# A gated graph update on one core: the new state as (1-z)n + zh, shared out over GpSimd, ScalarE and VectorE

## The reference, cut to what matters

```python
h = x
for i in range(4):
    hw = einsum('bnc,cd->bnd', h, weight[i])
    m  = einsum('bjn,bjd->bnd', adj, hw)
    gx = m @ w_ih[i].T + b_ih[i];  gh = h @ w_hh[i].T + b_hh[i]
    r = sigmoid(xr + hr);  z = sigmoid(xz + hz)
    n = tanh(xn + r * hn)
    h = (1 - z) * n + z * h
out = layernorm(x + h * mask[:, :, None])
```

## Time and profile before

| | us |
|---|---|
| median of 3 runs | 537.22 (536.68 to 537.37) |
| the profiled execution | 537.31 |
| its span (first to last instruction) | 535.5 |

### The profile page before, as it was taken

The page is one execution under the profiler, slowest core; times in us unless marked ns, Lnnn a source line. Parts: engine busy times, 40 slices in busy tenths (PEclk is TensorE's granted clock), DMA queues, the critical chain, the costliest instruction groups (busy, mean ns, idle before and its releaser), DMA issues.

```text
span 535.5 us, 7420 instructions
## 1 busy us (share of the span) xinstructions
PE 514.2 (96%) x2288; PEld 422.0 (79%) x2288; DVE 388.8 (73%) x678; ACT 383.8 (72%) x638; POOL 219.9 (41%) x162
## 2 busy tenths in 40 slices
PE   5999999999999999999999999999999999999970
PEld 4688888888888888888888888888888888888760
DVE  3787666666788886666689886667688887767595
ACT  4668777648776779956786877984986777985444
POOL 2045232344345454432336644332355454344443
PEclk9999999999999999999999999999999999999995
DMA  8951653265642356273662166356472165424212
GB/s 305 380 199 47 226 195 126 87 169 156 234 141 80 121 179 226 88 224 119 203 239 77 61 211 215 118 163 190 133 280 80 60 218 171 171 89 151 86 60 82
DMA packets 78896, 85.13 MB, mean 159 GB/s; under 512 B 3768, under 2 KB 61712, under 8 KB 78864
## 3 DMA queue, kind: packets, MB, share of 16 engines
q1 hardware_dynamic: 78864, 84.73, 47.9%
HBM read 64.27 MB, written 20.45 MB: 158 GB/s over the span
## 4 chain that ended last, share of the span: by engine, by line
PE 91%; SPq 2%; DMA 1%; POOL 1%; DVE 1%; issue 1%; ACT 1%; POOLq 0%; DVEq 0%; ACTq 0%
PE p_S L508 40%; PE p_r L522 5%; PE p_r L518 5%; PE p_r L519 5%; PE p_z L518 5%; PE p_z L522 5%; PE p_z L519 5%; PE p_hn L518 3%; PE p_hn L522 3%; PE p_hn L519 3%; PE p_xn L522 3%; PE p_xn L518 3%; PE p_xn L519 3%; DMA adj_in<-in_adj_dram 1%; PE p_tr L453 1%
## 5 line engine op out<-in xcount | busy, mean ns | idle before, releaser
L1272 POOL TENSOR_TENSOR work<-hT,work 128x512 f32<-128x512 f32 x63 | 86.6, 1375 | 266.7 <-ACT work L710 266.7
L508 PE MATMUL p_S<-adj_hi,nat_hi 128*128 128x512 f32 x480 | 187.4, 391 | 0.0
L508 PE MATMUL p_S<-adj_hi,nat_lo 128*128 128x512 f32 x480 | 186.8, 389 | 0.0
L508 PEld LDWEIGHTS p_S<-adj_hi,nat_hi 128*128 128x128 f32 x480 | 90.1, 188 | 18.9 <-DVE nat_lo L894 0.3
L508 PEld LDWEIGHTS p_S<-adj_hi,nat_lo 128*128 128x128 f32 x480 | 90.1, 188 | 18.5
L1141 DVE SCALAR_TENSOR_TENSOR work<-p_hn,bias,work 128x512 f32<-128x512 f32 x62 | 46.5, 750 | 79.3 <-ACT work L710 78.8
L1276 POOL TENSOR_TENSOR work<-work 128x512 f32<-128x512 f32 x63 | 90.1, 1430 | 4.9
L710 ACT ACTIVATE work<-p_r,bsum 128x512 f32<-128x512 f32 x63 | 43.4, 688 | 60.7 <-PE p_r L522 60.6
L931 DVE STREAM_TRANSPOSE work<-hT 128x512 f32<-128x512 f32 x62 | 69.2, 1116 | 2.1
L710 ACT ACTIVATE work<-work,bias 128x512 f32<-128x512 f32 x63 | 45.7, 725 | 31.0 <-DVE work L1145 28.6
L682 ACT ACTIVATE low_words<-adj_in 128x1024 bf16<-128x1024 uint16 x64 | 67.1, 1049 | 1.0
(11 more groups left out here) (148 smaller groups left out, 924.8 us busy)
## 6 DMA issues: line engine op xcount, KB each, us to landing
adj_in<-in_adj_dram SPq DMA_DIRECT2D x72, 512.0 KB, 6.7
bounce<-work SPq DMA_DIRECT2D x62, 256.0 KB, 2.0
low<-bounce SPq DMA_DIRECT2D x62, 256.0 KB, 2.8
x_in<-in_x_dram SPq DMA_DIRECT2D x8, 512.0 KB, 6.7
y<-in_x_dram SPq DMA_DIRECT2D x8, 512.0 KB, 4.4
out_dram<-y SPq DMA_DIRECT2D x7, 512.0 KB, 4.1
out_dram<-y SPq DMA_DIRECT2D x2, 256.0 KB, 2.7
y<-in_L_gnn_w_ih_dram SPq DMA_DIRECT2D x2, 192.0 KB, 7.4
```

What stands on the lines that cost most here:

```text
L508: last = nc.tensor.matmul(p_S[h][:, :], part[:, s, j], adj_hi[:, s, j, half(h)], start=(j == 0 and part is nat_hi), stop=(j == NB - 1 and ...
L1272: nc.gpsimd.tensor_tensor(t_sb[:, h], hT[:, s, half(h)], n_sb[:, h], ALU.subtract).then_inc(d_sub, 1)
```

## The change

In all steps but the last of the last pair, POOL makes zh (into `r_sb`, which is free after `t_mul`) as soon as z and t are there; ACT turns z into 1 - z in place, behind n and zh (`keep`, a Copy with scale -1 and bias 1); and DVE makes (1-z)n into `t_sb` and adds zh. The last step's half 0 keeps its three POOL operations, and one layer-norm power is issued after the loop instead of at its end.

```diff
+            def keep(p, k, h):
+                act.wait_ge(zh_made, HS * p + k + 1)
+                act.wait_ge(n_act, HS * p + k + 1)
+                nc.scalar.activation(z_sb[:, h], z_sb[:, h], ACT.Copy, bias=1.0, scale=-1.0).then_inc(z_kept, 1)
...
                         gate(n_sb[:, h], t_sb[:, h], t_add, n_act, ACT.Tanh, bias[:, 0, G * l + 2:G * l + 3], p, k)
+                        keep(p, k, h)
...
             def new_state(p, g, h):
-                dve.wait_ge(d_mul, HS * p + 2 * g + h + 1)
-                nc.vector.tensor_tensor(hT[:, g % 2, half(h)], n_sb[:, h], t_sb[:, h], ALU.add).then_inc(h_new, 1)
+                dve.wait_ge(z_kept, HS * p + 2 * g + h + 1)
+                nc.vector.tensor_tensor(t_sb[:, h], z_sb[:, h], n_sb[:, h], ALU.mult).then_inc(nz_made, 1)
+                dve.wait_ge(nz_made, HS * p + 2 * g + h + 1)
+                dve.wait_ge(zh_made, HS * p + 2 * g + h + 1)
+                nc.vector.tensor_tensor(hT[:, g % 2, half(h)], r_sb[:, h], t_sb[:, h], ALU.add).then_inc(h_new, 1)
...
-                        pool.wait_ge(n_act, HS * p + k + 1)
-                        nc.gpsimd.tensor_tensor(t_sb[:, h], hT[:, s, half(h)], n_sb[:, h],
-                                                ALU.subtract).then_inc(d_sub, 1)
-
-                        pool.wait_ge(d_sub, HS * p + k + 1)
-                        nc.gpsimd.tensor_tensor(t_sb[:, h], z_sb[:, h], t_sb[:, h],
-                                                ALU.mult).then_inc(d_mul, 1)
...
+                        pool.wait_ge(z_act, HS * p + k + 1)
+                        pool.wait_ge(t_mul, HS * p + k + 1)
+                        nc.gpsimd.tensor_tensor(r_sb[:, h], z_sb[:, h], hT[:, s, half(h)], ALU.mult).then_inc(zh_made, 1)
                     if g in (1, 2) and not first:
                         inverse_deviation(p - 1, g - 1)
-                    elif g == STEPS - 1 and last:
-                        inverse_deviation(p, 0)
 
             pairs(pool, body)
+            inverse_deviation(PAIRS - 1, 0)
```

More of the change, by code:

```diff
@@ L166, in gnn_kernel @@
         d_mul = sem("d_mul")
+        zh_made = sem("zh_made")
+        z_kept = sem("z_kept")
+        nz_made = sem("nz_made")
         h_new = sem("h_new")
@@ L1265, in body @@
                                                     hT_lo[:, s, half(h)].bitcast(F32), ALU.add).then_inc(xT_whole, 1)
-                    for h in range(1 if last and g == STEPS - 1 else 2):
+                    if last and g == STEPS - 1:
+                        pool.wait_ge(n_act, HS * p + 2 * g + 1)
+                        nc.gpsimd.tensor_tensor(t_sb[:, 0], hT[:, 1, half(0)], n_sb[:, 0], ALU.subtract).then_inc(d_sub, 1)
+                        pool.wait_ge(d_sub, 1)
+                        nc.gpsimd.tensor_tensor(t_sb[:, 0], z_sb[:, 0], t_sb[:, 0], ALU.mult).then_inc(d_mul, 1)
+                        pool.wait_ge(d_mul, 1)
+                        nc.gpsimd.tensor_tensor(hT[:, 1, half(0)], n_sb[:, 0], t_sb[:, 0], ALU.add).then_inc(h_new, 1)
+                        break
+                    for h in range(2):
                         k = 2 * g + h
```

## The result

The changed kernel takes 551.64 us (median of 3 runs, 551.37 to 552.01) against 537.22 before: the ratio is 1.0266 with a 95% interval of 1.0249 to 1.0283. The forecast of 549.0 was 2.6 us short, and its range of 540 to 556 holds the time. The profiled execution took 551.64 with a span of 549.8, which is 14.3 more than the 535.5 of before, at the same granted clock (0.988).

What follows compares the result with a forecast made beforehand. PE, busy 96% of the span, was taken as the bound, so lateness of DVE or ACT costs PE time. Terms 5.1 + 1.95 + 2.8 + 1.2 + 0.45 + 0.2 = 11.7 on 537.3 gave 549.0 us, range 540 to 556.

Steps and rivals of the forecast that it cites:

- the hold: DVE's `nat_lo`, with two SBUF inputs, stands behind POOL's running zh: 0.49 us lost for each half.
- A: Steps 4 and 5 of pairs 1 to 3, where ACT is full: 3 x 1.7 = 5.1 us, lower bound 2.7.
- B: Step 0 of pairs 1 to 3: one `keep` in ACT's gapless queue, 0.66 us a time, 1.95 in all.
- C: Step 1, no slack at `hT_lo`: 0.8 us in three pairs, 0.4 in pair 0, 2.8 in all.
- D: Steps 2 and 3 of pairs 1 to 3: DVE's additions against `S_lo`'s slack, 0.2 us a step, 1.2 in all.
- E: Step 7 of pairs 0 to 2: ACT late at `t_mul` of half 0, 0.15 us each, 0.45 in all.
- F: The end: longer `new_state`, and the residual before the last `S_lo` later but under POOL's operations as before: 0.2 us.
- My own case: The forecast's main case, the summed slowdown: 545.5 to 552.5 us, chance 0.50.
- Slack takes more: Rival: same places, but overlooked idle time in each queue absorbs more; 543 us, down to 538.4, chance 0.22.
- The relief on DVE decides: Rival: POOL leaves the residuals and PE's 3.0 us of DVE waits go; faster, 534.3 us, chance 0.07.
- Covered after all: Rival: DVE and ACT, some 80% busy, absorb the work and PE's waits stay; 537.3 us, chance 0.08.
- The power holds DVE: Rival: POOL's layer-norm power holds DVE's product and addition, making steps 2 and 3 cost 9.6; 557 us, chance 0.10.

Runs made afterwards that it cites:

- experiment 2: The changed kernel with the product (1-z)n made on POOL, so that DVE only adds: 542.07 us, ratio 1.009.
- experiment 3: The changed kernel with zh over 8 of 512 columns, most of zh left out, every wait kept: 543.83 us, ratio 1.0114.
- experiment 1: The changed kernel without the Copy on ACT; DVE makes (z-1)n in one instruction and subtracts it from zh: 547.58 us, ratio 1.0187.
- experiment 4: The kernel before with an in-place copy of z added on ACT behind every n: 541.57 us, ratio 1.008.
- experiment 7: The changed kernel without the Copy (DVE makes (z-1)n) and with zh over 8 of 512 columns: 538.84 us, ratio 1.0031.
- experiment 9: The kernel before with full zh added on POOL, its difference and product cut to 8 columns except in the last step: 537.31 us, ratio 1.0003.
- experiment 10: The changed kernel without the Copy (DVE makes (z-1)n), zh of half 1 waiting for the new state of half 0: 540.56 us, ratio 1.0059.
- experiment 5: The kernel before with two DVE moves: step 0's `measure` behind the first residual, the last step's `s_low` ahead of the second: 536.50 us, ratio 0.9994.
- experiment 8: The kernel before with full zh added on POOL ahead of its two old operations, unread, DVE's addition waiting for it: 557.57 us, ratio 1.0386.
- experiment 6: The changed kernel with the two DVE moves of experiment 5: 549.08 us, ratio 1.0224.
- experiment 11: The kernel of experiment 10 with the two DVE moves of experiment 5: 539.73 us, ratio 1.0047.

## Why the prediction was right, and where its terms were off

**The mechanism held.** The time is lost in the new waits that were named: for ACT's `S_hi` in steps 4 and 5 and for r in step 4, more for `t_mul` in step 0 and for `hT_lo` in step 1. Not named was a wait of 0.37 to 0.43 for `hT_lo` in step 0. PE has the same 2288 matmuls, but its busy time, said to be unchanged, is 8.5 us more: the aggregation's keep their mean of 0.391 and 0.389, while those behind the new waits are longer in the record (the one with `S_lo` into `p_r` 0.407 for 0.391). Experiments 2, 3 and 1 take away DVE's product, the hold and the Copy, one each, and give back 9.4, 7.6 and 3.9 of the 14.4 us.

**The prices.** The Copy took 0.63 (0.62 said), the product 0.68 (0.69), the residual of step 1 1.14 (1.13). The hold cost 0.60 instead of 0.49, 1.28 where 0.68 is usual, so that the mean of `nat_lo` is 1.26 and not 1.1 to 1.2. The 0.12 that I let be hidden is there: at `nat_lo`'s start zh still had 208.66 + 1.30 - 209.23 = 0.73 to run, and 0.60 of it was lost. What was off is zh's start. I had it 0.03 behind the end of `t_mul`; it came 0.14 behind (207.77 + 0.75 = 208.52 to 208.66).
The Trainium skill's rule of the whole instruction ("SBUF — State Buffer", section "SBUF: two separate sides") had made 0.61 out of my start. That is close to the 0.60 by chance: from the recorded start it gives 0.73, and the trace shows 0.13 less.

**A**, said 5.1, measured 5.63. Step 4 costs 1.00 to 1.03 instead of 1.25, step 5 0.82 to 0.90 instead of 0.45; that the sum is so near is in part luck, since one is too high and the other too low. The waits in the step 4 shown are 0.48, 0.43 and 0.50 against 0.6, 0.25 and 0.4; the step as a whole gets a part of them back. Step 5 was mis-sized: I took it for a remainder of step 4's lateness, but it has the full ACT queue and both new costs again (0.69 for `S_hi` and 0.43 for `S_lo` in pair 1).

**B**, said 1.95, measured 2.64. "One Copy in ACT's queue" was a cause but not the only one: experiment 4, the Copy alone, costs 1.86 there, and experiment 1, without it, 1.86 as well, by a later `take_xT` that puts `nat_lo<-x_in` under POOL's sum. Experiment 7, with neither, has 0.1. The Copy, or product with hold: either suffices, both together are little more. This step of the prediction was incomplete.

**C**, said 2.8, measured 3.10 (0.66, 0.87, 0.94, 0.63). The saving on the second residual is there (1.14 for 2.17), but the first state product is held by zh as well: it took 1.28 at 290.69. So is the first residual of step 0, 1.67 for 1.13, which the prediction didn't have; in pair 2 it costs nothing, since DVE waits 0.59 for ACT behind it.

**D**, said 1.2 over steps 2 and 3, measured 1.09, all of it in step 3 and none in step 2. **E**, said 0.45, measured 0.51.

**F**, said 0.2, measured 1.64, the term furthest off. 0.60 of it is a wait of 0.94 for `nat_lo` at the last step's start; the same step is as much longer in experiments 1, 2 and 9 (0.56 to 0.60), which have the hold, and no longer in 3, 4 and 7, which don't, nor in 10, where zh comes later. The other 1.04 came through a transfer. The residual ahead of the last `S_lo` waited for it, in DVE's timeline of the last step after:

```profile
530.76 1.14 DVE L957 SCALAR_TENSOR_TENSOR y<-low,mask,y 128x128 f32<-128x128 f32 x4 [3.21 <-DMA low<-bounce]
531.82 0.68 DVE L904 TENSOR_TENSOR S_lo<-p_S,S_hi 128x512 fp32r<-128x512 f32 x1
```

PE's wait for that `S_lo` is 2.83 for the 1.6 of the earlier trace rows. I had that residual as hidden under POOL's three operations, as before, and had the transfers as covered; this one isn't, because a DVE operation that PE waits for stands behind the residual.

**First step and start.** Pair 0's step 0 became 0.60 shorter, the start 0.31 longer: -0.3, not foreseen. It doesn't go with the change: step 0 there is 0.23 to 0.40 shorter in experiments 2, 3, 4, 7 and 9, and 0.24 longer in 10.

**What the sum hid.** I added the three prices at each place, less a slack. The slack is the point. Before, `S_hi` was ready at 213.31 for a load at 214.35, 1.04 of cover. The product's 0.7 alone fits under it, the hold's 0.6 alone too: in step 4 PE's loads wait once only, for r, 0.38 in experiment 7 and 0.24 in experiment 9. But 1.3 doesn't fit, and PEld's timeline in experiment 1 has three waits:

```profile
217.02 0.19 PEld L521 LDWEIGHTS p_r<-S_hi,wx_hi 128*128 128x128 f32 x1 [0.54 <-ACT S_hi L659]
217.75 0.19 PEld L525 LDWEIGHTS p_r<-S_lo,wx_hi 128*128 128x128 f32 x1 [0.43 <-DVE S_lo L903]
219.70 0.19 PEld L521 LDWEIGHTS p_r<-hT_hi,wh_hi 128*128 128x128 f32 x1 [0.50 <-issue]
```

Once `S_hi` is late at all, `S_lo` is late too, by 0.43 in every step 4 and 5 of pairs 1 to 3, here and in the kernel after, whether `S_hi` was late by 0.33 or by 0.70. Step 4 then costs 0.83 to 1.07, step 5 0.5. In step 1 the residual's saved 1.04 is the cover: product or hold alone costs nothing in pairs 1 and 2, both together 0.56 and 0.59. Over all pairs steps 4 and 5 are 4.2 of experiment 1's 10.5, steps 0 of pairs 1 to 3 1.9, steps 1 2.1, the last step and what follows it 2.2. So +1.8 and +0.3 make +10.5 mainly because covers are used up; the part at the end also has a late transfer. The Copy is different: alone it costs 0.45 to 0.71 in step 0, where DVE already stood idle for ACT. I think that with the slack kept apart from the prices A's step 5 would have shown itself; that is an opinion, not a result.

**The range.** My own case was given as 545.5 to 552.5. Its terms, A from 2.7 to 5.8 and a third on each of B to D, make 544.6 to 551.7, and 551.64 is at the upper edge of that: nearly every term was too low. In *Slack takes more*, 1.5 stands for B's 1.95 without a reason.

**The rivals.** *Slack takes more* (543) is refuted by A, B and C at or above their terms. *The relief on DVE decides* (534.3): the residual did get its 1.04 back, but no variant with the product on DVE comes below the kernel before. *Covered after all* is refuted. *The power holds DVE* (557) is refuted in place; POOL's timeline in the kernel after, in step 2 of pair 1:

```profile
199.12 2.01 POOL L1268 TENSOR_TENSOR rstd<-vare,mhalf 128x8 f32<-128x8 f32 x1 [4.42 <-DVE vare L981]
```

and DVE's:

```profile
199.67 0.69 DVE L1003 TENSOR_TENSOR hT<-work 128x512 f32<-128x512 f32 x1
```

The addition has two SBUF inputs, lies wholly under the power and takes its usual 0.69, and so it is at all six powers of steps 1 and 2. `z_rest`, which I had held against this rival, has a single input and was no test of it. The strict reading of the Trainium skill's rule ("SBUF — State Buffer", section "SBUF: two separate sides"), a hold for the whole length of a GpSimd instruction that reads SBUF, does not fit here, while it fits the multiplication of 512 columns but for 0.13.

**What stays open.** One `bounce` in the last step took 4.1 us from issue to landing. The view of that tile in the kernel after, from 500 to 530 us:

```profile
DMA to landing us min/median/max: 2.0/2.6/4.1
```

The same transfer, by the time from its issue to that of `low`, which waits for it, took 2.1 before, 2.1 to 2.2 in experiments 2, 4 and 9, 2.5 in 7, 3.1 and 3.2 in 5 and 8, and 3.6 to 4.4 in 1, 3, 6, 10 and 11. All from 3.6 up, the kernel after among them, have the product on DVE, but 5 and 8, with 3.1 and 3.2, don't, and 7 has it with 2.5. In the kernel after the bulk of it had moved by 525.4; from then until 527.4 the DMA engines moved at most 33 GB/s, where before nothing followed the bulk. What that trickle is wasn't looked into, so the cause is open, and with it whether F's 1.04 belongs to the change. Why `take_xT` is late enough in step 1 of experiment 10 to cost up to 0.36 wasn't traced either.

## What to carry to other kernels

Before you move an element-wise operation between engines, read for each consumer on the bound engine how early its operand is ready now; costs that each fit under that slack are nearly free singly (1.8 and 0.3 us here) and dear together (10.5), so price them as a sum against it and not one by one. When GpSimd works beside VectorE, look in the trace at what VectorE runs meanwhile, and not only at how long GpSimd works: moving one of the two 1.30 us operations of a step under the transpose, which has one input, took 7.0 us off experiment 1. And a term counted as "behind a stall, so nearly free" in one step has to be counted anew in the next step of the same kind.

## What the runs showed of the hardware that was not expected

- A VectorE operation with two SBUF inputs under a GpSimd multiplication of 128x512 is longer by what is left of that, all but 0.13: 0.60 of 0.73 for `nat_lo`, in the mean of 48 1.26 to 1.28 for 0.68 (after, experiments 1, 2 and 9). Four pieces of a residual took 4.44 for 1.11 under three operations in a row (experiment 7).
- GpSimd's power over 128x8, 2.0 us long, doesn't do that: 0.69 for the addition under it, six times of six.
- The transpose of 128x512 on VectorE, with one input, keeps its 1.12 under a GpSimd multiplication (experiment 10).
- In the kernel after, GpSimd's multiplication starts 0.14 to 0.18 behind the end of the VectorE operation that it waits for.
- The same 256 KB transfer to DRAM is followed by its reader after 2.1 to 2.2 us in four kernels and after 3.6 to 4.4 in six others, at the same point of the last step; in the kernel after its bulk had moved 2 us before the end.
